# VectorE takes the low half of u one step later, behind the next step's row maximum (cross-attention, 16 images, one core)

## The chip, the cores and the metric

One core of a Trainium2 chip runs the kernel. The metric is the device time in microseconds (us); a time is the median of several runs. Times inside the program are from one execution that the hardware profiler recorded.

## The reference, cut to what matters

```python
# N=16 images, c=64 channels, s=256 positions, context (64, 256), H=8 heads
xn = (input - mu) * rsqrt(var + EPS) * gamma + beta        # mean and variance over the whole image
q  = einsum('oc,ncs->nos', Wq, xn) + bq                    # 8 heads of 64
k, v = heads of einsum('od,nds->nos', Wkv, context) + bkv
att = softmax(einsum('nhqc,nhkc->nhqk', q*scale, k*scale)) # 256 x 256 for each head
y   = einsum('nhqk,nhkc->nhqc', att, v)
out = einsum('co,nos->ncs', Wo, y) + bo
return input + out
```

## The kernel before, in words

The weights are folded first: Wq with Wk (the matrix a), Wo with Wv (the matrix b_w). For one image the kernel makes t = a·xn, from which the scores are t·context, and u = context·b_w, the values with Wo already in them, for 8 heads at once. Numbers that must be more exact than one pass of TensorE gives are split: a high part, written by ScalarE from PSUM, and a low part, the PSUM value minus the high part, written by VectorE or GpSimd from the same bank. So t becomes t_a and t_b, u becomes u_hi and u_lo (fp16), and the softmax numerator p becomes p_hi and p_lo.

The order of the work is written out by hand. Each engine has its own in-order queue, and each builds it by the same loop over steps (n, h): n is the image whose scores are made, h = 0 to 7 the head. Step (n, h) stands for the whole work of one head, and what is made ahead or behind is placed into it:

- TensorE, in this order within a step: in even steps the sums of values of two heads that are four steps old (`av`, L479 to L481, 24 matmuls into ps_z); in steps 0 and 4 the products t for a later image (L497, L498); the scores of this head (L522, L523, four matmuls into ps_sc); the raw products for a row maximum, 11 steps ahead (L546, into ps_max, two banks); in step 1 the transpose of the finished output of image n-2 into ps_m (L557); in steps 3 and 7 one half of u for image n+1 into ps_m (L589, L590); in step 5 the transpose of the row maxima of image n+1 into ps_m (L458).
- ScalarE: t_a (L667), p_hi and p_full by Exp (L675, L678), then u_hi (L685) in steps 3 and 7, and in step 5 the copy of the transposed maxima (L648) with a small DMA into t_b (L658).
- VectorE: t_b (L878) in steps 1 and 5; in even steps the reciprocal of the sums (L888); the row maximum (L894); in even steps four operations that add to z_sum (L907, L910); in step 1 the output row x_res (L917); in steps 3 and 7 u_lo (L924), last; and p_lo for six of the last heads (L930).
- GpSimd: p_lo (L773). SyncE: the DMAs that copy parts of t_a, t_b, context and x between partitions.

ps_m is one bank of PSUM that four uses share in turn: half 0 of u in step 3, the transposed maxima in step 5, half 1 of u in step 7, the transposed output in step 1 of the next image. Each user waits until the bank was read. For two of them the reader is VectorE's u_lo:

```python
pe.wait_ge(dve_max, (m + 1) * H)                         # transpose of the maxima, step 5
pe.wait_ge(dve_ulo, 2 if m == 1 else 2 * m + 1)
...
pe.wait_ge(dve_ulo, 2 * (n + 1))                         # transpose of the output, step 1
```

The first 19 steps, n = -1 to (1, 2), follow tables of their own (U_FIRST and others): the four halves of u for images 0 and 1 are made in steps (0, 2), (0, 3), (0, 7) and (1, 0).

Of the kernel before, what the change touches and what calls it, by code (L numbers as in the profile page):

```python
# [25 lines left out]
N, C, S, H = 16, 64, 256, 8  # L26
# [52 lines left out]
def xattn_program(nc, x2_in, x_tiles_in, ctx2_in, wq_in, wk_in, w_in, out):  # L79
# [4 lines left out]
    with stack:  # L84
        def sb(name, shape, dt):
            return stack.enter_context(nc.sbuf_tensor(name, shape, dt))

        def ps(name, shape):
            return stack.enter_context(nc.psum_tensor(name, shape, fp32))

        def sem(name):
            return stack.enter_context(nc.semaphore(name))
# [21 lines left out]
        u_hi = sb("u_hi", [P, 2, KT, H, U_W], fp16)  # L114
        u_lo = sb("u_lo", [P, 2, KT, H, C], fp16)
# [43 lines left out]
        ps_m = ps("ps_m", [P, 512])  # L159
# [27 lines left out]
        dve_ulo, dve_y = sem("dve_ulo"), sem("dve_y")  # L187
        act_uhi, act_mt = sem("act_uhi"), sem("act_mt")
# [5 lines left out]
        def need(eng, s, count):  # L194

            if count > 0:
                eng.wait_ge(s, count)
# [89 lines left out]
        def u_at(n, h):  # L287

            if n < 1 or (n, h) < (1, 3):
                i = n * H + h  # L290
                return next(((e // 2, e % 2) for e, s in enumerate(U_FIRST) if s == i), None)
            return (n + 1, h // 4) if h in (3, 7) and 1 <= n < N - 1 else None

        def mt_at(n, h):

            if n < 1:
                i = n * H + h
                return next((((0, 0), (0, 1), (1, 0))[e] for e, s in enumerate(MT_FIRST) if s == i), None)
            return (n + 1, 0) if h == 5 and 1 <= n < N - 1 else None
# [107 lines left out]
        def _(pe):  # L407
# [52 lines left out]
            def step(n, h):  # L460
# [108 lines left out]
                if e := u_at(n, h):  # L569
                    m, kt = e  # L570
                    b, keys = m % C_BUFS, slice(kt * P, (kt + 1) * P)
                    if kt == 0:
                        c_ready(pe, m)
                        if m == 0:
                            pe.wait_ge(act_bhi, 1)
                            pe.wait_ge(dve_blo, 1)
                            pe.wait_ge(dve_ones, 3)
                            pe.wait_ge(act_mt, 2)
                        elif m == 1:
                            pe.wait_ge(act_mt, 3)  # L580
                        elif m == 2:
                            pe.wait_ge(dve_ulo, 4)
                        else:
                            pe.wait_ge(dve_y, m - 2)
                    elif m < 2:
                        pe.wait_ge(dve_ulo, 2 * m + 1)
                    else:
                        pe.wait_ge(act_mt, m + 2)
                    mm(ps_m[:], c_seq[:, b, 0, keys], b_w[:, 0, :], start=True, stop=False)  # L589
                    mm(ps_m[:], c_seq[:, b, 1, keys], b_w[:, 1, :], start=False, stop=True).then_inc(pe_u, 1)  # L590
# [8 lines left out]
        def _(act):  # L599
# [61 lines left out]
            def step(n, h):  # L661
# [18 lines left out]
                if e := u_at(n, h):  # L680
                    m, kt = e
                    act.wait_ge(pe_u, 2 * m + kt + 1)
                    need(act, pe_av, (m - 1) * H)
                    act.wait_ge(pool_u1, 1)
                    nc.scalar.activation(u_hi[:, m % 2, kt, :, 0:C], ps_m[:].rearrange("p (h c) -> p h c", h=H), ACT.Copy).then_inc(act_uhi, 1)  # L685
# [94 lines left out]
        def _(dve):  # L780
# [67 lines left out]
            def step(n, h):  # L848
# [33 lines left out]
                if z_step:  # L882
                    m, first = z_step
# [6 lines left out]
                for m, unit in max_at(n, h):  # L890
# [3 lines left out]
                    nc.vector.tensor_reduce(to, ps_max[:, unit % 2, :].rearrange("p (t s) -> p t s", t=KT), X,  # L894
                                            ALU.max, negate=True).then_inc(dve_max, 1)

                if z_step:
                    m, first = z_step
                    dve.wait_ge(dve_inv, m * PAIRS + pair + 1)
                    if first == 0:  # L900
                        need(dve, pe_y, m - 1)
                    for k in range(2):
                        head = first + k
                        for qt in range(KT):
                            total, part, scale = z_sum[:, m % 2, qt, :], sums[:, qt, k, 0:C], inv_sum[:, pair % 2, qt * 2 + k:qt * 2 + k + 1]
                            if head == 0:
                                nc.vector.tensor_scalar(total, part, scale, 0.0, ALU.mult, ALU.add).then_inc(dve_zsum, 1)  # L907
                            else:
                                dve.wait_ge(dve_zsum, (m * H + head - 1) * KT + qt + 1)
                                nc.vector.scalar_tensor_tensor(out=total, in0=part, scalar=scale, in1=total, op0=ALU.mult,  # L910
                                                               op1=ALU.add).then_inc(dve_zsum, 1)

                if h == 1 and n >= 2:
                    m = n - 2
# [2 lines left out]
                    nc.vector.scalar_tensor_tensor(out=x_res[:, m:m + 1, :], in0=ps_m[:, 0:P].rearrange("p (o s) -> p o s", o=1),  # L917
                                                   scalar=u_unscale[:], in1=x_res[:, m:m + 1, :], op0=ALU.mult,
                                                   op1=ALU.add).then_inc(dve_y, 1)

                if e := u_at(n, h):
                    m, kt = e
                    dve.wait_ge(act_uhi, 2 * m + kt + 1)
                    nc.vector.tensor_tensor(u_lo[:, m % 2, kt, :, :], ps_m[:].rearrange("p (h c) -> p h c", h=H), u_hi[:, m % 2, kt, :, 0:C],  # L924
                                            ALU.subtract).then_inc(dve_ulo, 1)

                if n * H + h in LO_ON_VECTOR:
                    dve.wait_ge(act_p, n * H + h + 1)
# [2 lines left out]
                                            p_hi[:, h % P_BUFS, :, :].rearrange("p t s -> p (t s)"), ALU.subtract).then_inc(dve_plo, 1)  # L931

            run(step)


# [34 lines left out]
```

## Time and profile before

| what | value |
|---|---|
| median of 3 runs | 230.24 us (229.52 to 231.55) |
| span of the profiled execution, first to last instruction | 228.2 us |
| own time of the profiled execution | not recorded apart from the runs; the span is 2.0 us under their median |
| TensorE matmul busy | 208.6 us, 91% |
| VectorE busy | 199.3 us, 87% |
| ScalarE busy | 181.1 us, 79% |
| GpSimd busy | 160.3 us, 70% |
| clock granted to TensorE | lower in slices 3 to 5 and 7 of 40; from the eighth on nine tenths or more, but in the last slice |

The span is the time between the first and the last instruction of the program. Busy shares are averages over the whole span; a matmul counts as busy from start to modelled end, and matmuls overlap, so that its share is above what its work takes. From about 66 us on the program is periodic, one image in some 11.8 us.

### The profile page before, as it was taken

How to read it: one execution, taken by the hardware profiler on the slowest of the kernel's cores; microseconds unless marked ns; L12 is line 12 of the kernel's file. 1: busy time of each engine (PE TensorE's matmuls, PEld its weight loads, DVE VectorE, ACT ScalarE, POOL GpSimd, SP SyncE). 2: the span in 40 equal slices, each digit the busy share in tenths (PEclk: the TensorE clock that was granted, in tenths of full speed). 3: DMA queues.
4: the chain of work that ended last, by engine and by line, in shares of the span. 5: the costliest groups of instructions: out<-in, count | busy, mean ns of one | idle time of the engine just before them, and what ended most of it. 6: DMA issues, size and time to landing. Idle time of an engine off the chain costs nothing.

```text
span 228.2 us, 7194 instructions
## 1 busy us (share of the span) xinstructions
PE 208.6 (91%) x2511; PEld 179.9 (79%) x2511; DVE 199.3 (87%) x589; ACT 181.1 (79%) x371; POOL 160.3 (70%) x157
## 2 busy tenths in 40 slices
PE   6968878799999999999999998999999999999872
PEld 6857757588888798889888887888888888887761
DVE  3589987879898999899999999999999998989765
ACT  2374586787889988898889888989897979888880
POOL 5135185777987877789788887789686869776460
PEclk9975897999999999999999999999999999999998
DMA  5964137480767566566665665656657656442000
GB/s 134 261 272 93 27 82 174 107 184 14 164 141 160 131 153 142 132 141 151 140 153 122 160 151 121 151 127 154 142 127 166 149 133 143 93 94 62 13 3 23
DMA packets 31090, 29.04 MB, mean 127 GB/s; under 512 B 4240, under 2 KB 29840, under 8 KB 31056
## 3 DMA queue, kind: packets, MB, share of 16 engines
q1 hardware_dynamic: 30224, 28.07, 52.4%
q10 hardware_dynamic: 832, 0.53, 1.0%
q8 instruction: 20, 0.33, 0.6%
q14 instruction: 14, 0.11, 0.2%
HBM read 3.80 MB, written 1.05 MB: 21 GB/s over the span
## 4 chain that ended last, share of the span: by engine, by line
PE 41%; POOL 20%; issue 13%; ACT 11%; DVE 11%; ACTq 2%; POOLq 0%; DVEq 0%
POOL p_lo L773 19%; PE ps_sc L522 6%; PE ps_max L546 6%; PE ps_sc L523 5%; PE ps_z L479 4%; ACT p_full L678 4%; DVE neg_max L894 4%; ACT p_hi L675 3%; PE ps_z L481 3%; PE ps_z L480 3%; PE ps_z L414 3%; PE ps_m L589 2%; PE ps_t L497 2%; PE ps_m L590 2%; DVE z_sum L910 2%
## 5 line engine op out<-in xcount | busy, mean ns | idle before, releaser
L773 POOL TENSOR_TENSOR p_lo<-p_full,p_hi 128x512 f16<-128x512 f32 x122 | 139.9, 1163 | 42.3 <-ACT p_full L678 41.2
L675 ACT ACTIVATE p_hi<-ps_sc 128x512 f16<-128x512 f32 x128 | 77.9, 608 | 18.3 <-PE ps_sc L523 15.9
L894 DVE TENSOR_REDUCE neg_max<-ps_max 128x2 f32<-128x512 f32 x128 | 85.9, 677 | 6.9 <-PE ps_max L546 6.8
L678 ACT ACTIVATE p_full<-ps_sc 128x512 f32<-128x512 f32 x128 | 78.7, 615 | 0.0
L522 PE MATMUL ps_sc<-t_a,c_seq 128*128 128x256 f32 x256 | 71.2, 300 | 3.5 <-issue 2.6
L523 PE MATMUL ps_sc<-t_b,c_seq 65*128 65x256 f32 x256 | 67.3, 284 | 0.0
L479 PEld LDWEIGHTS ps_z<-u_hi,p_hi 128*128 128x128 f16 x512 | 46.4, 97 | 12.8 <-issue 8.2
L479 PE MATMUL ps_z<-u_hi,p_hi 128*128 128x65 f16 x512 | 53.0, 195 | 2.2 <-DVE p_lo L930 1.9
L522 PEld LDWEIGHTS ps_sc<-t_a,c_seq 128*128 128x128 f32 x256 | 49.2, 192 | 5.9 <-issue 4.6
L480 PE MATMUL ps_z<-u_lo,p_hi 128*128 128x64 f16 x512 | 52.8, 193 | 0.0
L481 PE MATMUL ps_z<-u_hi,p_lo 128*128 128x65 f16 x512 | 52.7, 194 | 0.0
L523 PEld LDWEIGHTS ps_sc<-t_b,c_seq 65*128 65x128 f32 x256 | 49.0, 191 | 2.2
L546 PE MATMUL ps_max<-c_pad,t_a 128*128 128x512 f32 x120 | 49.0, 415 | 0.8 <-DVE neg_max L894 0.4
L910 DVE SCALAR_TENSOR_TENSOR z_sum<-ps_z,inv_sum,z_sum 128x64 f32<-128x64 f32 x224 | 48.4, 277 | 0.2
L480 PEld LDWEIGHTS ps_z<-u_lo,p_hi 128*128 128x128 f16 x512 | 46.6, 98 | 0.1
L481 PEld LDWEIGHTS ps_z<-u_hi,p_lo 128*128 128x128 f16 x512 | 46.6, 97 | 0.0
L924 DVE TENSOR_TENSOR u_lo<-ps_m,u_hi 128x512 f16<-128x512 f32 x32 | 22.0, 688 | 9.9 <-ACT u_hi L685 9.7
L546 PEld LDWEIGHTS ps_max<-c_pad,t_a 128*128 128x128 f32 x120 | 22.7, 192 | 4.0 <-DVE neg_max L894 2.8
L667 ACT ACTIVATE t_a<-ps_t 128x512 fp32r<-128x512 f32 x30 | 18.2, 607 | 5.8 <-PE ps_t L498 5.8
L685 ACT ACTIVATE u_hi<-ps_m 128x512 f16<-128x512 f32 x32 | 20.1, 629 | 1.1 <-PE ps_m L590 1.1
L878 DVE TENSOR_TENSOR t_b<-ps_t,t_a 128x512 fp32r<-128x512 f32 (+1 forms) x30 | 20.4, 680 | 0.0
L497 PE MATMUL ps_t<-x_seq,a_hi 128*128 128x256 f32 x60 | 18.4, 327 | 1.1 <-ACT x_seq L628 1.1
(108 smaller groups left out, 233.9 us busy)
## 6 DMA issues: line engine op xcount, KB each, us to landing
t_a<-t_a SPq DMA_DIRECT2D x90, 128.0 KB, 2.4
t_b<-t_b SPq DMA_DIRECT2D x30, 128.0 KB, 2.5
x_seq<-x_hi SPq DMA_DIRECT2D x15, 128.0 KB, 2.4
c_pad<-c_hi SPq DMA_DIRECT2D x30, 64.0 KB, 2.1
c_seq<-c_hi SPq DMA_DIRECT2D x15, 128.0 KB, 2.4
x_res<-x_tiles SPq DMA_DIRECT2D x4, 256.0 KB, 6.7
out<-x_res SPq DMA_DIRECT2D x16, 64.0 KB, 2.0
x_seq<-x_lo SPq DMA_DIRECT2D x15, 64.0 KB, 2.1
```

The costliest lines, as they stand in the source:

```text
L479: mm(ps_z[:, bank, z0:z0 + Z_W], p_hi[:, buf, kt, qs], u_h, start=(kt == 0), stop=False)
L480: mm(ps_z[:, bank, z0:z0 + C], p_hi[:, buf, kt, qs], u_l, start=False, stop=False)
L481: last = mm(ps_z[:, bank, z0:z0 + Z_W], p_lo[:, buf, kt, qs], u_h, start=False, stop=(kt == KT - 1))
L497: mm(bank[:, j * S:(j + 1) * S], a_hi_cols[:, first:first + 2 * C], x_seq[:, q, 0, :], start=True, stop=False)
L522: mm(ps_sc[:, bank, kt * S:(kt + 1) * S], c_seq[:, b, 0, keys], t_a[:, q, head, :], start=True, stop=False)
L523: last = mm(ps_sc[:, bank, kt * S:(kt + 1) * S], c_seq[0:C + 1, b, 1, keys], t_b[0:C + 1, q, head, :], start=False, stop=True)
L546: last = mm(ps_max[:, bank, :], t_a[:, q, head, qt * P:(qt + 1) * P], c_pad[:, q, :, :].rearrange("p k s -> p (k s)"), start=True, stop=True)
L675: nc.scalar.activation(p_hi[:, buf, :, :].rearrange("p t s -> p (t s)"), scores, ACT.Exp).then_inc(act_phi, 1)
L678: nc.scalar.activation(p_full[:, head % 2, :], scores, ACT.Exp).then_inc(act_p, 1)
L773: nc.gpsimd.tensor_tensor(p_lo[:, buf, :, :].rearrange("p t s -> p (t s)"), p_full[:, head % 2, :], p_hi[:, buf, :, :].rearrange("p t s -> ...
L894: nc.vector.tensor_reduce(to, ps_max[:, unit % 2, :].rearrange("p (t s) -> p t s", t=KT), X, ALU.max, negate=True).then_inc(dve_max, 1)
L910: nc.vector.scalar_tensor_tensor(out=total, in0=part, scalar=scale, in1=total, op0=ALU.mult, op1=ALU.add).then_inc(dve_zsum, 1)
```

## The change

VectorE's u_lo leaves the end of its step. For the 14 images 2 to 15, both halves, it moves into the next step: the one of step 3 to step 4, the one of step 7 to step 0 of the next image. There it stands behind the reciprocal and the row maximum and ahead of the four sums of values. For the four halves of the start (images 0 and 1) the step stays the same, but the place within it is the new one, which in steps (0, 7) and (1, 0) is ahead of the sums in place of behind them. No instruction is added or removed, and no wait is changed.

```diff
+        def u_low_at(n, h):
+
+            if n * H + h < H + 3:
+                return u_at(n, h)
+            i = n * H + h - 1
+            return u_at(*divmod(i, H)) if h in (0, 4) else None
+
...
                     nc.vector.tensor_reduce(to, ps_max[:, unit % 2, :].rearrange("p (t s) -> p t s", t=KT), X,
                                             ALU.max, negate=True).then_inc(dve_max, 1)
 
+                if e := u_low_at(n, h):
+                    m, kt = e
+                    dve.wait_ge(act_uhi, 2 * m + kt + 1)
+                    nc.vector.tensor_tensor(u_lo[:, m % 2, kt, :, :], ps_m[:].rearrange("p (h c) -> p h c", h=H), u_hi[:, m % 2, kt, :, 0:C],
+                                            ALU.subtract).then_inc(dve_ulo, 1)
+
                 if z_step:
                     m, first = z_step
                     dve.wait_ge(dve_inv, m * PAIRS + pair + 1)
...
-
-                if e := u_at(n, h):
-                    m, kt = e
-                    dve.wait_ge(act_uhi, 2 * m + kt + 1)
-                    nc.vector.tensor_tensor(u_lo[:, m % 2, kt, :, :], ps_m[:].rearrange("p (h c) -> p h c", h=H), u_hi[:, m % 2, kt, :, 0:C],
-                                            ALU.subtract).then_inc(dve_ulo, 1)
```

VectorE's queue from step 7 of one image to step 1 of the next, before (pe_s1 is counted by TensorE's products for the row maximum, pe_av by the sums of values, act_uhi by u_hi, act_thi by t_a, pe_y by the transpose of the output; dve_ names are VectorE's own):

```order
L894 TENSOR_REDUCE neg_max<-ps_max 128x2 [waits pe_s1]
L924 TENSOR_TENSOR u_lo<-ps_m,u_hi 128x512 [waits act_uhi]
L888 RECIPROCAL inv_sum<-ps_z 128x4 [waits pe_av]
L894 TENSOR_REDUCE neg_max<-ps_max 128x2 [waits pe_s1]
L910 SCALAR_TENSOR_TENSOR z_sum<-ps_z,inv_sum,z_sum 128x64 [waits dve_zsum,dve_inv]
L910 SCALAR_TENSOR_TENSOR z_sum<-ps_z,inv_sum,z_sum 128x64 [waits dve_zsum] x3
L878 TENSOR_TENSOR t_b<-ps_t,t_a 128x2x256 [waits act_thi]
L894 TENSOR_REDUCE neg_max<-ps_max 128x2 [waits pe_s1]
L917 SCALAR_TENSOR_TENSOR x_res<-ps_m,u_unscale,x_res 128x128 [waits pool_xb,pe_y]
```

The same stretch of VectorE's queue after the change (line numbers of the changed kernel: L901 is the row maximum, L907 u_lo, L895 the reciprocal, L923 the sums, L885 t_b, L930 x_res):

```order
L901 TENSOR_REDUCE neg_max<-ps_max 128x2 [waits pe_s1]
L895 RECIPROCAL inv_sum<-ps_z 128x4 [waits pe_av]
L901 TENSOR_REDUCE neg_max<-ps_max 128x2 [waits pe_s1]
L907 TENSOR_TENSOR u_lo<-ps_m,u_hi 128x512 [waits act_uhi]
L923 SCALAR_TENSOR_TENSOR z_sum<-ps_z,inv_sum,z_sum 128x64 [waits dve_zsum,dve_inv]
L923 SCALAR_TENSOR_TENSOR z_sum<-ps_z,inv_sum,z_sum 128x64 [waits dve_zsum] x3
L885 TENSOR_TENSOR t_b<-ps_t,t_a 128x2x256 [waits act_thi]
L901 TENSOR_REDUCE neg_max<-ps_max 128x2 [waits pe_s1]
L930 SCALAR_TENSOR_TENSOR x_res<-ps_m,u_unscale,x_res 128x128 [waits pool_xb,pe_y]
```

u_lo moved past the reciprocal and the row maximum of step 0 and still stands ahead of t_b and the row maximum of step 1. From step 3 to step 5 it is the same, before:

```order
L894 TENSOR_REDUCE neg_max<-ps_max 128x2 [waits pe_s1]
L924 TENSOR_TENSOR u_lo<-ps_m,u_hi 128x512 [waits act_uhi]
L888 RECIPROCAL inv_sum<-ps_z 128x4 [waits pe_av]
L894 TENSOR_REDUCE neg_max<-ps_max 128x2 [waits pe_s1]
L907 TENSOR_SCALAR z_sum<-ps_z,inv_sum 128x64 [waits pe_y,dve_inv]
```

and after the change:

```order
L901 TENSOR_REDUCE neg_max<-ps_max 128x2 [waits pe_s1]
L895 RECIPROCAL inv_sum<-ps_z 128x4 [waits pe_av]
L901 TENSOR_REDUCE neg_max<-ps_max 128x2 [waits pe_s1]
L907 TENSOR_TENSOR u_lo<-ps_m,u_hi 128x512 [waits act_uhi]
L920 TENSOR_SCALAR z_sum<-ps_z,inv_sum 128x64 [waits pe_y,dve_inv]
```

Here u_lo moved behind the row maximum of step 4, the last one that the transpose of step 5 needs. The queues of the other engines are as they were.

## Rows read from the trace of the kernel before

**Rows 1.** The page: busy us, share of the span, instructions

```profile
PE 208.6 (91%) x2511; PEld 179.9 (79%) x2511; DVE 199.3 (87%) x589; ACT 181.1 (79%) x371; POOL 160.3 (70%) x157
```

**Rows 2.** Who waited for whom, whole span: us in total, times, longest us

```profile
ACT p_hi L675 <- PE ps_sc L523: 15.9, 30, 1.7
DVE u_lo L924 <- ACT u_hi L685: 9.7, 15, 1.5
...
DVE neg_max L894 <- PE ps_max L546: 6.8, 21, 1.1
...
PEld ps_m L458 <- DVE neg_max L894: 6.0, 15, 0.7
```

**Rows 3.** The chain of waits, 106 to 114.2 us: start us, us, what

```profile
106.83 0.58 DVE u_lo L924
...
109.55 0.61 DVE neg_max L894
...
110.20 0.50 PE ps_max L546
...
114.05 0.28 PE ps_m L458
```

**Rows 4.** VectorE in time order: start us, us, instruction, [idle before, releaser]

```profile
100.68 0.69 DVE L924 TENSOR_TENSOR u_lo<-ps_m,u_hi 128x512 f16<-128x512 f32 x1
...
101.63 0.69 DVE L894 TENSOR_REDUCE neg_max<-ps_max 128x2 f32<-128x512 f32 x1 [0.17 <-PE ps_max L546]
102.24 0.47 DVE L907 TENSOR_SCALAR z_sum<-ps_z,inv_sum 128x64 f32<-128x64 f32 x2
...
105.63 0.68 DVE L894 TENSOR_REDUCE neg_max<-ps_max 128x2 f32<-128x512 f32 x1
106.83 0.69 DVE L924 TENSOR_TENSOR u_lo<-ps_m,u_hi 128x512 f16<-128x512 f32 x1 [0.51 <-ACT u_hi L685]
...
107.52 0.66 DVE L894 TENSOR_REDUCE neg_max<-ps_max 128x2 f32<-128x512 f32 x1
```

**Rows 5.** TensorE in time order, image 6

```profile
101.19 0.40 PE L546 MATMUL ps_max<-c_pad,t_a 128*128 128x512 f32 x1
...
102.38 0.28 PE L458 MATMUL ps_m<-ident,neg_max 128*16 128x128 f32 x1
...
105.91 0.36 PE L497 MATMUL ps_t<-x_seq,a_hi 128*128 128x256 f32 x1
...
106.94 0.40 PE L546 MATMUL ps_max<-c_pad,t_a 128*128 128x512 f32 x1
...
107.89 0.27 PE L557 MATMUL ps_m<-ident,z_sum 128*128 128x128 f32 x1
...
112.87 0.40 PE L546 MATMUL ps_max<-c_pad,t_a 128*128 128x512 f32 x1
```

**Rows 6.** TensorE's weight load ahead of the row maximum of step 3

```profile
110.20 0.19 PEld L546 LDWEIGHTS ps_max<-c_pad,t_a 128*128 128x128 f32 x1 [0.26 <-DVE neg_max L894]
```

**Rows 7.** ScalarE at step 6 of the same image

```profile
104.24 0.60 ACT L675 ACTIVATE p_hi<-ps_sc 128x512 f16<-128x512 f32 x1 [0.68 <-PE ps_sc L523]
```

**Rows 8.** TensorE: step 0 and 1 of image 2, then transposes for images 3 and 15

```profile
60.00 0.39 PE L546 MATMUL ps_max<-c_pad,t_a 128*128 128x512 f32 x1
60.23 0.27 PE L557 MATMUL ps_m<-ident,z_sum 128*128 128x128 f32 x1
...
66.49 0.28 PE L458 MATMUL ps_m<-ident,neg_max 128*16 128x128 f32 x1
...
208.54 0.28 PE L458 MATMUL ps_m<-ident,neg_max 128*16 128x128 f32 x1 [0.49 <-DVE neg_max L894]
```

**Rows 9.** VectorE at the start, step (1, 0)

```profile
47.47 0.85 DVE L910 SCALAR_TENSOR_TENSOR z_sum<-ps_z,inv_sum,z_sum 128x64 f32<-128x64 f32 x4
48.24 0.69 DVE L924 TENSOR_TENSOR u_lo<-ps_m,u_hi 128x512 f16<-128x512 f32 x1
```

**Rows 10.** VectorE at the last u_lo

```profile
212.78 0.69 DVE L924 TENSOR_TENSOR u_lo<-ps_m,u_hi 128x512 f16<-128x512 f32 x1 [1.54 <-ACT u_hi L685]
```

## The prediction

> **What bounds the kernel now.** I read the totals first, then the table of who waited for whom, the chain, and last the timelines of two engines over one image. Four engines are busy for 70% to 91% of the span [rows 1], so the shares do not name the bound. The table of waits shows that they hold each other in turn: VectorE waits 9.7 us for u_hi ahead of u_lo, ScalarE 15.9 us for scores, VectorE 6.8 us for the products of the row maximum, and TensorE's weight load 6.0 us, in 15 places, ahead of the transpose of the maxima [rows 2]. The last is one wait for each image from 1 to 15, always for VectorE's last row maximum.
>
> The chain gives the loop. ScalarE's u_hi releases u_lo at 106.83 [rows 4]; from there it stays on VectorE up to the row maximum of step 1 at 109.55, which releases TensorE's products for step 3 at 110.20; it stays on TensorE until VectorE's row maximum of step 4, and reaches the transpose of the maxima at 114.05 [rows 3]. After that transpose come TensorE's next scores, for which ScalarE waits 0.68 us [rows 7], and ScalarE's queue leads to u_hi again. One turn takes 114.05 - 102.38 = 11.67 us [rows 3, 5], and from the transpose at 66.49 to the one at 208.54 [rows 8] there are 12 turns, 142.05 us, 11.84 us each.
>
> How much of a turn does TensorE need for itself? I cut it at the two places where it reads ps_m, the transpose of the maxima (step 5) and the transpose of the output (step 1). From the first at 102.38 to the products for the maximum of step 0 at 106.94: 4.56 us. From there to the transpose of the output at 107.89: 0.95. From that to the products of step 4 at 112.87: 4.98, of which some 0.21 is a wait for VectorE [rows 5, 6] (the weight load sat idle for 0.26); the wait's restart costs something too, so I take 4.60 us, as an estimate between 4.5 and 4.8. From the products of step 4 to the transpose of the maxima: 1.19 (101.19 to 102.38). Sum 11.30 us: TensorE waits some 0.4 us in a turn and is close to the bound. So is VectorE. Whatever adds a wait of TensorE behind VectorE's queue adds it to the turn.
>
> **The change, part by part.** Nothing is added, so only the order of VectorE's queue counts. The maximum takes 0.61 us of the queue (101.63 to 102.24); u_lo, with the same recorded 0.69 us, the same; u_lo with the reciprocal behind it 0.69 (106.83 to 107.52) [rows 4].
>
> *The wait that goes.* u_lo no longer stops VectorE until u_hi is there. In this image that was 0.51 us [rows 4]. Behind the next maximum, u_hi has long ended. So VectorE could be up to 0.5 us earlier at step 0. But the maximum of step 0 needs TensorE's products: they start at 106.94 and VectorE can start at the earliest 0.44 us later (101.19 to 101.63, where VectorE did wait for them) [rows 4, 5], at 107.38; before it started at 107.52. What is gained there is 0.14 us. The wait moves, from u_hi to TensorE's products.
>
> *Step 3 to 4.* Here u_lo did not wait (100.68), and the maximum behind it still waited 0.17 us for TensorE's products [rows 4]. u_lo filled time in which VectorE had nothing else. Moved behind the maximum, it leaves that gap empty, and is late itself: it starts where the sums started, at 102.24.
>
> *First gate, the transpose of the maxima.* TensorE waits there for the last maximum already; it starts 0.75 us after that maximum does on VectorE (101.63 to 102.38) [rows 4, 5]. The bank ps_m is read by u_lo, and the transpose waits for that too. Before, u_lo was ahead of the maximum and cost nothing. Now it is behind it: the transpose comes 0.61 us later, products of step 4 + 0.44 + 0.61 + 0.75 = 1.80 us in place of 1.19. Queued behind it on TensorE are the sums of values, the scores of step 6 and everything else.
>
> *Second gate, the transpose of the output.* It waits for the other u_lo. Before, u_lo started at 106.83 and the transpose at 107.89 [rows 4, 5] had no wait. Now: products of step 0, then 0.44 to the start of the maximum, 0.61 for the maximum, 0.75 for u_lo and the release: again 1.80 us in place of 0.95. The cover is gone, since only one row of products and one head's scores lie between.
>
> Is VectorE free when the products of step 0 come? From the start of the maximum of step 4 to that of step 7 it needs 4.00 us without a gap (101.63 to 105.63) [rows 4]; add 0.69 for u_lo and the reciprocal and 0.61 for that maximum: 5.30. TensorE's products of step 0, with the lag, come at 0.61 + 0.75 + 4.56 + 0.44 = 6.36. VectorE waits about 1 us, so the gate goes by TensorE's products plus two VectorE operations, not by VectorE's load.
>
> *Sum for a turn.* 4.56 + 1.80 + 4.60 + 1.80 = 12.76 us against 11.84: +0.92. TensorE's old waits are already taken out in the 4.60, so the 0.44 + 0.21 that it waited before are given back. Twelve turns: +11.0.
>
> *The ends.* Image 2: products of step 0 at 60.00, and the transpose of the maxima for image 3 at 66.49, 6.49 us [rows 8]; after: 1.80 + 4.60 + 1.80 = 8.20, +1.7. In the last image the products t are absent, which the 12.76 counts; t and the four matmuls of the scores take 105.91 to 106.94 together, 1.03 us [rows 5], so t some half of it: -0.5. At the start, in steps (0, 7) and (1, 0), u_lo goes ahead of the sums (47.47 and 48.24 change places [rows 9]); the sums, t_b and what follows are up to 0.77 us later there, and the halves of u that wait for the bank are earlier. Bounds -0.8 and +0.8; I take +0.2, since u_hi is only just there at 48.24 and VectorE's next maximum then comes later. At the end the last u_lo waited 1.54 us for u_hi [rows 10], and its low part of p can go ahead now: -0.2, bounds -0.6 and +0.4.
>
> *The rest that moves with it.* The sums and t_b start 0.61 us later behind their maximum. t_b of step 1 is followed by the maximum of step 1, which TensorE's products of step 3 wait for; in the new turn TensorE is itself 0.85 us later there, so this wait goes away. SyncE's copies of t_b wait for it, several steps ahead of their use: nothing. GpSimd and ScalarE get more idle time, nothing of theirs is moved.
>
> Total: 11.0 + 1.7 - 0.5 + 0.2 - 0.2 = +12.2 us. Span 228.2 + 12.2 = 240.4. The runs' median lies 2.0 us above the span (230.24); the profiled execution has no time of its own on record, so I keep this distance: **242.4 us**, 5.3% slower.
>
> **The rivals.**
>
> *VectorE is the bound, and its gap closes.* Busy for 87% of the span, it waits 9.7 us for u_hi [rows 1, 2]. If the order of u_lo mattered to nobody, up to 1.2 us of the start excepted, some 8 us would come off: 222 us. Against it: at step 4 VectorE waits for TensorE right behind u_lo [rows 4], and the transpose of the maxima waits in each image for VectorE [rows 2]. It decides if the transposes do not in fact wait for u_lo's new place. Chance 0.04. A rule of the Trainium skill points this way: the page Perfetto Trace Analysis, section Identifying Performance Opportunities, says that one improves the most-contended engine, by its occupancy, and finds the gaps on it and what blocks them. By that rule the change closes the right gap. The rows here show that the engine with the gap is waited for at another place of its queue, and I go by them.
>
> *Only one gate bites.* If the transpose of the output does not wait (the products of step 0 come much earlier than the rest, or u_lo starts sooner), a turn is 4.56 + 0.95 + 4.60 + 1.80 = 11.91, and the kernel takes 231 to 233 us. If only the transpose of the output waits, 12.15 and 235. For it: the two gates were never both closed in the old trace. Against: both waits are in the code, and both distances come from idle engines. Chance 0.10, 234 us.
>
> *More than the two gates.* The image that I cut up took 11.67 us, the mean 11.84; what made others longer (copies of x on ScalarE, a late DMA ahead of step 0) may stay: 12 times 0.17 is 2 us, 244.5, which I count to the forecast. If in some images a third wait appears, or the granted clock falls in the new gaps, 248. Chance 0.06.
>
> *The change does nothing.* The order of VectorE's queue shows it moved; what could be is that the new waits eat just what the old ones gave. The gate sums differ by 0.9 us in a turn, too much for that. It is within the one-gate case.
>
> **How the numbers follow.** Forecast 0.80, with times of 239 to 245.5 (0.92 plus or minus 0.2 in 12 turns is 2.4 us, the ends plus or minus 1, the longer images on top); one gate 0.10; more 0.06; faster 0.04. The range is the forecast's, stretched a little to the one-gate case: 238 to 246. A measurement of this kernel tells about 1% from no change (its runs lie within 0.9%). Faster by over 1%: 0.04. Within 1%: 0.04, the lower end of the one-gate case. Slower by over 1%: 0.92.
>
> **What would show each step.** In the new profile: VectorE's wait of u_lo for u_hi all but gone (under 2 us in total, all in the first and last steps); its wait of the row maximum for TensorE's products up from 6.8 to 20 to 30 us, in 28 or more places of about 1 us; TensorE waiting for u_lo ahead of both transposes, some 0.8 us each in 14 images; VectorE's and TensorE's busy time unchanged; a turn of 12.7 to 12.8 us. The prediction is wrong if the transpose of the output starts 0.95 us behind the products of step 0 still, or if the turn stays under 12.2 us. If the turn comes out at 13 or more, something else waits that I left out: the DMA of the maxima ahead of step 0, or GpSimd's low parts.

## The result, and the profile after

The changed kernel takes 243.65 us (median of 4 runs, 242.59 to 245.42), the kernel before in the same session 229.88 us (229.22 to 231.55): ratio 1.0595, 95% interval 1.0521 to 1.0669. It is slower by 6%. The forecast was 242.4 us, range 238 to 246. The profiled execution took 243.1 us, its span 241.3 us, 13.1 us more than before. Runs of one kernel fall into a faster and a slower kind: a time given here is the median of all runs, a ratio is of the faster kind alone, and the executions profiled for `e5_late_tr`, `e7_late_sums`, `e10_old_tr_sums`, `e11_old_tr_sums2` and `e12_late_tr_sums2` were of the slower kind.

The page of the changed kernel, busy time, share of the span and instructions:

```profile
PE 206.2 (85%) x2511; PEld 179.7 (74%) x2511; DVE 199.8 (83%) x589; ACT 182.9 (76%) x371; POOL 160.3 (66%) x157
```

Busy times are those of [rows 1] to within 1.2%; the 13 us are idle time on every engine. Who waited for whom, whole span (us in total, times, longest us):

```profile
POOL p_lo L780 <- ACT p_full L685: 54.1, 60, 2.6
ACT p_hi L682 <- PE ps_sc L530: 30.2, 33, 1.3
DVE neg_max L901 <- PE ps_max L553: 25.6, 30, 1.3
PEld ps_m L465 <- DVE neg_max L901: 14.9, 15, 1.2
...
PE ps_m L465 <- DVE u_lo L907: 10.7, 14, 1.0
PE ps_m L564 <- DVE u_lo L907: 9.8, 13, 0.8
...
DVE u_lo L907 <- ACT u_hi L692: 2.1, 3, 0.8
```

Against [rows 2]: VectorE's wait for u_hi fell from 9.7 to 2.1 us, the three that are left are in the start. Its wait for the products of the row maximum rose from 6.8 to 25.6 us. So what the change takes from one wait of VectorE goes into another. TensorE waits 20.5 us for u_lo, 27 times, ahead of the two transposes; before it did so once, for 0.6 us, near the end. TensorE's timeline over one turn (start us, us, instruction, idle before and releaser); L553 are the products of the row maximum, L465 the transpose of the maxima, L564 that of the output:

```profile
105.08 0.27 PE L465 MATMUL ps_m<-ident,neg_max 128*16 128x128 f32 x1 [0.76 <-DVE u_lo L907]
...
109.80 0.40 PE L553 MATMUL ps_max<-c_pad,t_a 128*128 128x512 f32 x1
...
111.67 0.30 PE L564 MATMUL ps_m<-ident,z_sum 128*128 128x128 f32 x1 [0.76 <-DVE u_lo L907]
...
116.32 0.40 PE L553 MATMUL ps_max<-c_pad,t_a 128*128 128x512 f32 x1
...
118.20 0.27 PE L465 MATMUL ps_m<-ident,neg_max 128*16 128x128 f32 x1 [0.76 <-DVE u_lo L907]
```

The four parts of the turn, the counterparts of [rows 5], are 4.72, 1.87, 4.65 and 1.88 us: 13.12 in this turn. Over twelve turns, from the transpose at 66.31 to the one at 221.52, the mean is 12.93 us, with 1.86 to 1.88 from the products to the transpose at both places in each of them:

```profile
66.31 0.27 PE L465 MATMUL ps_m<-ident,neg_max 128*16 128x128 f32 x1 [0.76 <-DVE u_lo L907]
...
221.52 0.27 PE L465 MATMUL ps_m<-ident,neg_max 128*16 128x128 f32 x1 [1.00 <-DVE u_lo L907]
```

VectorE at the second gate:

```profile
109.03 0.17 DVE L895 RECIPROCAL inv_sum<-ps_z 128x4 f32<-128x4 f32 x1
110.23 0.69 DVE L901 TENSOR_REDUCE neg_max<-ps_max 128x2 f32<-128x512 f32 x1 [1.03 <-PE ps_max L553]
110.84 0.68 DVE L907 TENSOR_TENSOR u_lo<-ps_m,u_hi 128x512 f16<-128x512 f32 x1
111.44 0.85 DVE L923 SCALAR_TENSOR_TENSOR z_sum<-ps_z,inv_sum,z_sum 128x64 f32<-128x64 f32 x4
112.20 0.68 DVE L885 TENSOR_TENSOR t_b<-ps_t,t_a 128x512 fp32r<-128x512 f32 x1
112.80 0.68 DVE L901 TENSOR_REDUCE neg_max<-ps_max 128x2 f32<-128x512 f32 x1
```

and ScalarE's u_hi that this u_lo reads:

```profile
108.75 0.63 ACT L692 ACTIVATE u_hi<-ps_m 128x512 f16<-128x512 f32 x1
```

The reciprocal is done, u_hi has been there since 109.38, and VectorE is idle for 1.03 us with u_lo behind the maximum that it waits to make. That is the mechanism: u_lo was ready to run in the idle time and stands behind an instruction that is not.

### The profile page after: what moved, and what is told of

Its sections match the earlier page's. It is cut to its first block, busy times and chain, and to the rows that moved or that the text cites. A ratio compares the mean times of both kernels' runs of the same rounds, so it can differ in the third digit from the quotient of the medians.

```text
span 241.3 us, 7194 instructions
## 1 busy us (share of the span) xinstructions
PE 206.2 (85%) x2511; PEld 179.7 (74%) x2511; DVE 199.8 (83%) x589; ACT 182.9 (76%) x371; POOL 160.3 (66%) x157
## 4 chain that ended last, share of the span: by engine, by line
PE 66%; DVE 14%; issue 10%; ACT 7%; ACTq 1%; POOL 0%; POOLq 0%
PE ps_sc L529 10%; PE ps_sc L530 9%; DVE u_lo L907 9%; PE ps_max L553 8%; PE ps_z L486 7%; PE ps_z L488 6%; PE ps_z L487 6%; PE ps_t L504 3%; PE ps_m L596 3%; PE ps_m L597 3%; PE ps_z L421 3%; PE ps_t L505 3%; ACT p_full L685 2%; PE ps_m L564 2%; PE ps_m L465 2%
## 5 line engine op out<-in xcount | busy, mean ns | idle before, releaser
L901 DVE TENSOR_REDUCE neg_max<-ps_max 128x2 f32<-128x512 f32 x128 | 86.2, 680 | 25.7 <-PE ps_max L553 25.6
L923 DVE SCALAR_TENSOR_TENSOR z_sum<-ps_z,inv_sum,z_sum 128x64 f32<-128x64 f32 x224 | 48.2, 274 | 0.2
L553 PE MATMUL ps_max<-c_pad,t_a 128*128 128x512 f32 x120 | 47.6, 404 | 0.3 <-DVE neg_max L901 0.2
L553 PEld LDWEIGHTS ps_max<-c_pad,t_a 128*128 128x128 f32 x120 | 22.7, 192 | 1.1 <-DVE neg_max L901 1.0
L907 DVE TENSOR_TENSOR u_lo<-ps_m,u_hi 128x512 f16<-128x512 f32 x32 | 21.8, 680 | 2.1 <-ACT u_hi L692 2.1
L885 DVE TENSOR_TENSOR t_b<-ps_t,t_a 128x512 fp32r<-128x512 f32 (+1 forms) x30 | 20.3, 678 | 0.0
```

Source lines behind the costliest of these rows:

```text
L553: last = mm(ps_max[:, bank, :], t_a[:, q, head, qt * P:(qt + 1) * P], c_pad[:, q, :, :].rearrange("p k s -> p (k s)"), start=True, stop=True)
```

## The experiments

In each, "before" is the kernel before, run on the same chip in the same session. Twelve kernels were run. A regular turn is one of the shortest length that recurs; in each kernel some turns are longer.

**One half late at a time.** `e1_half0` takes only the half of step 3 late, `e2_half1` only that of step 7. The other stays at the end of its own step.

```diff
             i = n * H + h - 1
-            return u_at(*divmod(i, H)) if h in (0, 4) else None
+            return u_at(*divmod(i, H)) if h == 4 else None      # e2_half1: h == 0
+
+        def u_low_same_step(n, h):
+
+            return u_at(n, h) if n * H + h >= H + 3 and h == 7 else None   # e2_half1: h == 3
```

> Only the half of u of step 3 is taken late (in step 4, behind the maximum); the half of step 7 stays at the end of its step. Two gates: the transpose of the maxima comes 1.87 us behind its products as in the changed kernel, the transpose of the output 0.95 us behind its products as before, and VectorE still waits for u_hi in step 7. A turn of 4.6 + 0.95 + 4.95 + 1.87 = 12.35 us, time 238 to 240 us. Rival, VectorE's order as such (the sums and t_b come later): half of the whole loss, 236.8 us, with no wait at the transpose of the maxima beyond the old one.

> Only the half of step 7 is taken late (in step 0 of the next image); the half of step 3 stays. Two gates: 4.6 + 1.87 + 4.6 + 1.19 = 12.25 us a turn, time 234 to 236 us, TensorE waits some 0.8 us ahead of the transpose of the output and not for u_lo ahead of the transpose of the maxima. Rival, VectorE's order as such: half of the whole loss, 236.8 us, as the other half alone.

Measured: e1_half0 236.28 us, ratio 1.0285 (1.0220 to 1.0351); e2_half1 235.08 us, ratio 1.0254 (1.0176 to 1.0333). The first is below its expectation of 238 to 240 us, the second inside its own. The times do not separate the two theories; the traces do. In e1_half0 a regular turn is 12.26 us (4.58 + 0.95 + 4.86 + 1.87), in e2_half1 12.21 (4.56 + 1.87 + 4.60 + 1.18). The waits, first e1_half0:

```profile
PE ps_m L469 <- DVE u_lo L911: 10.7, 14, 1.0
...
DVE u_lo L941 <- ACT u_hi L696: 6.0, 13, 2.0
```

then e2_half1:

```profile
PE ps_m L568 <- DVE u_lo L911: 9.2, 13, 0.8
```

L469 is the transpose of the maxima there, L568 that of the output. Each half makes its own transpose wait, and only that one. Twelve turns last 148.13 and 148.25 us against 142.05 before: +6.1 and +6.2, both together in the changed kernel +13.2. The two gates add up to within 0.9 us.

**The place behind the maximum, with and without.** `e3_ahead_max` has u_lo in the next step too, but ahead of the row maximum; `e4_behind_sums` has it another four operations later, behind the sums.

```diff
+                if e := u_low_at(n, h):            # e3_ahead_max: here, ahead of the row maximum
+                    ...
                 for m, unit in max_at(n, h):
                     ...
-                if e := u_low_at(n, h):
-                    ...
                 if z_step:
                     ...
+                if e := u_low_at(n, h):            # e4_behind_sums: here, behind the sums
+                    ...
                 if h == 1 and n >= 2:
```

> u_lo in the next step as in the changed kernel, but ahead of the row maximum (behind the reciprocal). Two gates: it is the place behind the maximum that costs, so this is the kernel before again but for the start: 229 to 231.5 us, a turn of 11.7 to 11.9. Rival, that a step later is too late whatever stands ahead of it: 243 us or a good part of the way there.

> u_lo another 0.76 us later, behind the four sums of values of the next step. Two gates: each transpose comes 0.76 us later still, 2.63 us behind its products, a turn of 14.4 us, 28 times 0.76 is 21 us on top of the changed kernel: 262 to 266 us. Rival, that the loss comes from the sums and t_b standing behind u_lo: they are earlier here than in the changed kernel, so 243 us or less.

Measured: e3_ahead_max 232.19 us, ratio 1.0126 (1.0063 to 1.0190); e4_behind_sums 264.26 us, ratio 1.1497 (1.1409 to 1.1586). In e3_ahead_max the turns are those of before (twelve of them 141.25 us); its 2 to 3 us were lost ahead of the first regular turn, where its transpose for image 3 starts at 69.46 against 66.49. The expectation, up to 231.5 us, left that out. The trace shows where it goes: in the start u_lo keeps its step, so that it now stands ahead of a maximum in the step in which u_hi is made, and waits 1.06, 2.37 and 2.26 us for it (0.46, 0.74 and nothing in the kernel before), with TensorE's products waiting up to 1.8 us behind. VectorE waits 11.6 us for u_hi in all. e4_behind_sums is a dose, the same delay made larger: the parts of a turn that are not gates are 4.58 and 4.59 us, as in most turns of the changed kernel, and both gates are 2.64 us, 0.77 more than in the changed kernel, just the four sums. The turn is 14.44 us. TensorE in that kernel:

```profile
111.13 0.27 PE L465 MATMUL ps_m<-ident,neg_max 128*16 128x128 f32 x1 [1.53 <-DVE u_lo L923]
```

The rival that the delay of the sums is what costs is out for the changed kernel: in e4_behind_sums the sums are not behind u_lo, and it is 20 us slower. It does not test t_b, which stands behind u_lo there too; `e7_late_sums` below does.

**The transposes out of the gates' way.** If the two gates are all of it, moving both transposes on TensorE behind the next 24 matmuls should fill the waits. `e5_late_tr` does this to the changed kernel, `e6_old_tr` to the kernel before.

```diff
                 if e := av_at(n, h):
                     ...
+                if h == 2 and n >= 2:              # was: h == 1, behind the products of the row maximum
+                    ...
+                    nc.tensor.transpose(ps_m[:, 0:P], z_sum[:, m % 2, :, :].rearrange("p t c -> p (t c)"), ident[:]).then_inc(pe_y, 1)
+
+                if n >= 1 and h == 6 and (e := mt_at(n, 5)):   # was: at the end of step 5
+                    transpose_max(*e)
+
                 for turn, m, k in t_at(n, h):
```

> The changed kernel with both transposes into ps_m moved on TensorE: from the end of step 5 and step 1 to behind the sums of values of step 6 and step 2 (24 matmuls, 0.71 us later in TensorE's queue). u_lo is as late as in the changed kernel. Two gates: the waits of 0.76 us are filled with the sums of values; a turn of 11.4 to 11.8 us, time 226 to 231 us. Rival, that u_lo's late place costs through VectorE's own queue: 240 us or more still.

> The kernel before with the same move of the two transposes, as the control. The wait of some 0.2 us ahead of the transpose of the maxima goes, VectorE's wait for u_hi stays: 226 to 230 us. If it is as fast as the late one with moved transposes, taking u_lo late gives nothing even with its price removed; if it is slower, the wait for u_hi was worth removing.

Measured: e5_late_tr 239.27 us, ratio 1.0332 (1.0214 to 1.0450), e6_old_tr 229.44 us, ratio 0.9981 (0.9933 to 1.0028). The first falls outside my expectation and comes close to the rival's 240 us: with the idle time of the gates filled, u_lo's late place still costs, through VectorE's own queue. TensorE's idle time ahead of the transposes is down to 0.8 us in all, 2 times, and the turn is still 12.71 us. In its place stands another wait, TensorE's products of step 3 and step 7 for VectorE's maximum two steps earlier: ps_max has two banks, and the maximum must have read its bank before new products go there. VectorE from the maximum of step 0:

```profile
109.54 0.69 DVE L904 TENSOR_REDUCE neg_max<-ps_max 128x2 f32<-128x512 f32 x1 [0.94 <-PE ps_max L565]
110.15 0.68 DVE L910 TENSOR_TENSOR u_lo<-ps_m,u_hi 128x512 f16<-128x512 f32 x1
110.75 0.85 DVE L926 SCALAR_TENSOR_TENSOR z_sum<-ps_z,inv_sum,z_sum 128x64 f32<-128x64 f32 x4
111.51 0.68 DVE L888 TENSOR_TENSOR t_b<-ps_t,t_a 128x512 fp32r<-128x512 f32 x1
112.11 0.68 DVE L904 TENSOR_REDUCE neg_max<-ps_max 128x2 f32<-128x512 f32 x1
```

and TensorE, the products of step 0, those of step 3, and those of step 4:

```profile
109.10 0.40 PE L565 MATMUL ps_max<-c_pad,t_a 128*128 128x512 f32 x1
...
112.85 0.50 PE L565 MATMUL ps_max<-c_pad,t_a 128*128 128x512 f32 x1 [0.37 <-DVE neg_max L904]
...
115.51 0.40 PE L565 MATMUL ps_max<-c_pad,t_a 128*128 128x512 f32 x1
```

A second loop: products, maximum, u_lo, sums, t_b, maximum, 109.10 to 112.85, 3.75 us, then 2.66 us of TensorE to the products of step 4, where the same begins again. The other half takes 3.74 and 2.56 us, together 12.71 us, the turn. VectorE is never idle between the two maxima. u_lo lengthened this loop by 0.6 us in each half as well; the gates, 0.2 us a turn longer, hid it.

The gates themselves are not open. The transpose of the output here:

```profile
110.75 0.19 PE L488 MATMUL ps_z<-u_hi,p_lo 128*128 128x65 f16 x1
110.98 0.30 PE L498 MATMUL ps_m<-ident,z_sum 128*128 128x128 f32 x1
```

It starts 0.83 us after u_lo (110.15) and 1.88 us after the products of step 0, as in the changed kernel, 0.23 us behind a matmul of a row whose matmuls follow each other at 0.03. The trace's idle column says nearly nothing of it, since the matmuls of that row are recorded with 0.19 us each and the column counts from their modelled end.

**Each loop on its own.** To shorten the second loop, the four sums leave it: VectorE takes them one step later, behind the row maximum of the odd step, from step (2, 4) on. `e7_late_sums` is the changed kernel with this alone, `e8_late_tr_sums` with the moved transposes as well; `e9_old_sums` and `e10_old_tr_sums` are the same on the kernel before.

```diff
+                i = n * H + h
+                if 20 <= i < 116 and i % 2 == 0:
+                    z_step = None
+                elif 20 < i < 116:
+                    z_step = av_at(*divmod(i - 1, H))
+                    ...
                 if z_step:
                     m, first = z_step
                     dve.wait_ge(dve_inv, m * PAIRS + pair + 1)
```

> The changed kernel with VectorE's four sums of values one step later, behind the row maximum of the next (odd) step, from step (2, 4) to (14, 3); the two transposes stay. The chain on VectorE from the maximum of step 0 or 4 over u_lo and t_b to the maximum of step 1 or 5 is 0.76 us shorter. Two gates: nothing changes, a turn of 12.9 us, 242 to 245 us. Rival, the longer VectorE chain is what bounds the changed kernel: 235 us or less.

> Late u_lo, transposes behind the sums of values of step 6 and 2 (as in the run with both transposes moved), and VectorE's four sums one step later. If a second path, VectorE's maximum, u_lo, sums, t_b, maximum (3.75 us to TensorE's products two or three steps on), kept the turn at 12.7 us once the transposes were moved, it is now 0.76 us shorter and the turn comes to 11.3 to 11.6 us: 224 to 230 us. Rival, something else kept it there: 236 us or more.

> The kernel before with VectorE's four sums one step later. The old loop from u_hi over u_lo, the maximum, the sums, t_b and the next maximum to TensorE is 0.76 us shorter; TensorE's own 11.3 us and the 0.2 us wait at the transpose of the maxima are left: a turn of 11.4 to 11.6 us, 225 to 229 us. If TensorE's own work or ScalarE bounds the turn, 229 to 231.

> The kernel before with the transposes moved and the sums one step later: a turn of 11.3 to 11.5 us, 224 to 228 us. Beside the same with u_lo late it shows what late u_lo is worth with both of its prices removed: up to 0.1 us a turn in its favour, or nothing.

Measured: e7_late_sums 244.75 us, ratio 1.0656 (1.0553 to 1.0759); e8_late_tr_sums 233.74 us, ratio 1.0180 (1.0089 to 1.0271); e9_old_sums 229.29 us, ratio 1.0045 (1.0001 to 1.0090); e10_old_tr_sums 230.31 us (226.39 to 231.54), from which no ratio could be formed. The first lies inside its expectation, the other three miss theirs (224 to 230, 225 to 229 and 224 to 228 us). With the gates in place the shorter second loop gives nothing: in e7_late_sums the regular turn is 12.91 to 12.93, both gates 1.87. A late t_b is not what costs either: here it starts one maximum and one u_lo (1.2 us) after the start of the maximum of its step, in the kernel before one maximum and four sums (1.4 us). With the transposes moved the shorter loop gives 0.7 us a turn: 12.71 becomes 12.03 to 12.05. So the gates bound the changed kernel, and the second loop is right behind. But e8_late_tr_sums did not reach the 11.3 to 11.6 that I expected, and in e9_old_sums and e10_old_tr_sums the shorter turns are 11.5 to 11.7 us, as before. All three show a wait that my edit had made. In e8_late_tr_sums:

```profile
PE ps_m L599 <- DVE x_res L942: 4.5, 10, 0.5
```

L599 is u of step 3, which waits until x_res has read ps_m; in step 1 I had put the sums ahead of x_res. In e10_old_tr_sums this row is 1.9 us, 7 times, in e9_old_sums only 0.3 us, once. More of it shows at the weight load of u, whose idle time the trace puts down to no releaser: 9.2, 6.6 and 5.3 us in 12 or 13 places in e8, e10 and e9, against 1.4 us in one place in the kernel before and in the two kernels that follow.

**The two versions with that mended.** x_res goes ahead of the postponed sums in step 1 (from image 3 to 14). `e11_old_tr_sums2` has u_lo at its old place, `e12_late_tr_sums2` late; both have the moved transposes and the postponed sums.

```diff
+                if h == 1 and 3 <= n < 15:
+                    ...                          # x_res, ahead of the postponed sums
                 i = n * H + h
                 if 20 <= i < 116 and i % 2 == 0:
...
-                if h == 1 and n >= 2:
+                if h == 1 and n >= 2 and not 3 <= n < 15:
```

> u_lo at its old place; the transposes moved behind the sums of values of step 6 and 2, VectorE's sums one step later, and now the output row x_res ahead of those sums in step 1, since in the run with the sums ahead of it TensorE's u of step 3 waited for x_res (6.6 us in all). If that wait held the turn at 11.65 us, it now comes to 11.3 to 11.5: 224 to 228 us and 1% to 2% faster than before. Rival, TensorE's and ScalarE's own work or the start and end hold it: no change from before.

> The same with u_lo late. Here VectorE's maximum, u_lo and the transpose stand in front of x_res; TensorE's u of step 3 waited 4.5 us in all for x_res with the sums ahead of it. Without that: a turn of 11.4 to 11.7 us, 226 to 230 us. If late u_lo gives something once all its prices are gone, it is as fast as or faster than the same with u_lo at its old place; I expect it to be the same or 1% slower.

Measured: e11_old_tr_sums2 226.00 us, ratio 0.9888 (0.9847 to 0.9929); e12_late_tr_sums2 227.08 us, ratio 0.9830 (0.9768 to 0.9892). The second ratio rests on four of its twelve runs; the medians of all runs, beside 229.17 us for the kernel before, give 0.986 and 0.991. So both are faster than the kernel before, by 1% to 2%, and not apart from each other. Their regular turns are 11.2 to 11.3 and 11.4 us (over twelve turns 11.53 and 11.59). In e12_late_tr_sums2 the waits that the change had made or moved are small:

```profile
DVE neg_max L904 <- PE ps_max L565: 10.5, 30, 0.8
...
DVE u_lo L910 <- ACT u_hi L695: 2.7, 4, 0.8
...
PE ps_m L465 <- DVE u_lo L910: 0.8, 2, 0.5
```

The turn of 11.43 us in e12_late_tr_sums2 is still that of the gates. TensorE there, and VectorE's u_lo:

```profile
112.75 0.40 PE L565 MATMUL ps_max<-c_pad,t_a 128*128 128x512 f32 x1
...
114.39 0.20 PE L488 MATMUL ps_z<-u_hi,p_lo 128*128 128x65 f16 x1
114.62 0.27 PE L465 MATMUL ps_m<-ident,neg_max 128*16 128x128 f32 x1
```

```profile
113.79 0.68 DVE L910 TENSOR_TENSOR u_lo<-ps_m,u_hi 128x512 f16<-128x512 f32 x1
```

The transpose starts 0.83 us after u_lo and 1.87 us after the products; a regular turn is 3.77 + 1.87 + 3.93 + 1.87 us. In e11_old_tr_sums2 the same transpose follows the sums of values at 0.03 us, and the two stretches are 1.68 and 1.78:

```profile
114.07 0.20 PE L481 MATMUL ps_z<-u_hi,p_lo 128*128 128x65 f16 x1
114.10 0.27 PE L458 MATMUL ps_m<-ident,neg_max 128*16 128x128 f32 x1
```

In e11_old_tr_sums2 VectorE still waits 9.4 us for u_hi, and is no slower for it. So removing that wait is worth nothing measurable here even with its prices mostly paid otherwise. What both kernels have over the kernel before is that TensorE no longer stands idle for VectorE at the transposes, at the products of step 3 and 7, and at u; neither the moved transposes alone (e6_old_tr) nor the postponed sums alone (e9_old_sums) were faster, nor both without the new place of x_res (e10_old_tr_sums).

## Why the prediction was right, point by point

- *The wait that goes.* Right: 9.7 to 2.1 us, where under 2 was forecast. *It moves to TensorE's products:* right, 25.6 us in 30 places; forecast were 20 to 30.
- *The two gates.* Right in place and nearly in size: forecast 1.80 us at each, measured 1.87 in every turn. The term off is the release: I took 0.75 us from the start of u_lo to the transpose, as for the maximum; it is 0.83 (110.84 to 111.67). The dose of e4_behind_sums and the separate halves show that the gates cause it.
- *TensorE's own parts.* 4.56 and 4.60 forecast; 4.57 to 4.84 (4.63 on average) and 4.58 to 4.66 measured. The second was 4.98 before, so the old wait in it cost 0.38 us, not the 0.21 read off; the estimate of 4.60 had taken that in. The turn came to 12.93, outside the 12.7 to 12.8 that the prediction named as its sign. Twelve turns gave +13.2 us where the terms +11.0 and -0.5 stood: 1.7 of the 2.7 us between are the gates' 0.07, 24 times, and 0.9 the first part.
- *VectorE is free in time.* Right: it is idle for 1.03 us ahead of the maximum of step 0.
- *Image 2, +1.7 us.* Wrong. The products at 60.00 in [rows 8] are those of step 1, not of step 0; in these first steps the maxima still follow their table. u_lo stands ahead of that maximum (it starts at 58.53, the maximum at 59.74), and the transpose of the output follows its products at once in the changed kernel as well (59.30 and 59.54). From these products to the transpose for image 3 it is 7.01 us after, 6.49 before: +0.5, one gate instead of two.
- *Start, +0.2.* It gained: the same products come at 59.30 instead of 60.00, -0.7. In step (1, 0) u_lo started at 47.02 instead of 48.24, which the bounds allowed for and my value did not. *The end, -0.2:* +0.1 measured (19.78 against 19.67 us from the last transpose of the maxima on).
- The sum: 13.2 + 0.5 - 0.7 + 0.1 = 13.1 us of span, forecast 12.2. The turns were forecast 2.7 us too short in all, image 2 1.2 us too long and the start 0.9 us, and these largely cancel. That the total came within 1 us is in part luck; that it is near 243 us is not, since the turns alone give +13.2. The rest of the difference to 243.65 is within the runs.
- *What I had not seen* is the second loop. The prediction said of the wait of step 3's products only that it goes away; it does, but with the transposes moved it comes back at 12.7 us a turn. The changed kernel's time does not depend on it. The case "only one gate bites" was priced too low too, by the size of the gate: 11.91 and 12.15 forecast, 12.26 and 12.21 in e1_half0 and e2_half1. In the first the old wait of the products of step 3 is still there, 4.86 in place of 4.60.

What remains open: what bounds e11_old_tr_sums2, and why some turns in it and in e12_late_tr_sums2 take 11.8 to 12.1 us. The second loop and x_res were tried only together with other edits in the kernels that gained, so their shares of the gain are not known apart.

## What to carry to other kernels

An instruction that waits in an in-order queue may be filling idle time: before moving it behind another, look whether that other one waits too, and who reads the bank or buffer that it frees. Price the new place from the producer of the instruction that it now follows (here products + release + two VectorE operations), not from the wait that is saved. When one loop is cut, look for the next: here gates of 12.9 us a turn, a VectorE loop of 12.7, a wait for x_res at 12.0, and the gates again at 11.4 once the transposes had moved, lay behind one another, and only the kernels without the first three were faster. And an idle column near nothing does not show that a wait is gone: compare the distance from the start of the releasing instruction.

## What the runs showed of the hardware

- The same transpose starts 0.75 us after the start of the VectorE maximum that releases it (kernel before, 101.63 to 102.38), and 0.82 to 0.83 us after the start of the u_lo that does (at every gate of the changed kernel but the last, 0.80), though both operations are recorded with 0.68 to 0.69 us. Its weight load starts just ahead of it in both kernels, so it did not run ahead while the matmul waited for u_lo, although the trace names the maximum as its releaser:

```profile
102.37 0.09 PEld L458 LDWEIGHTS ps_m<-ident,neg_max 128*16 128x16 f32 x1 [0.39 <-DVE neg_max L894]
```

```profile
118.17 0.09 PEld L465 LDWEIGHTS ps_m<-ident,neg_max 128*16 128x16 f32 x1 [1.05 <-DVE neg_max L901]
```

  Why the release takes 0.08 us longer behind u_lo was not tried.
- TensorE waits of 0.76 us twice in 12.9 us left the granted clock at its upper level: it is 1.00 of full speed in each stretch of 24 us from 60 us to 204 us, before and after.
